# Edge stage of a graph network: edge features transposed in 32x32 squares by VectorE, sources broadcast by DMA

## The chip, the cores and the metric

The kernel runs on 1 core of one Trainium2 chip. The metric is the device time of one execution in microseconds (us). Of the kernel before, three runs are shown: 1167.19, 1169.51 and 1170.66 us, median 1169.51.

## What is computed

One layer of a graph network over 50,000 nodes with 128 features and 12,500 edges, in fp32. Every edge has a source `src` (the node that it adds to), a `dst` (the node that it reads), and 3, 5 and 32 features. Cut to what matters, with `idx_i = src` and `idx_j = dst`:

```python
h = relu(layernorm(x))
xx, xs, xp, xd = resmlp_0(h), resmlp_1(h)[idx_j], resmlp_2(h)[idx_j], resmlp_3(h)[idx_j]
gs, gp, gd = rbf @ w_rs, (rbf @ w_rp) * pij, (rbf @ w_rd) * dij      # rbf: 32 features, pij: 3, dij: 5
s = xx + segment_sum(gs * xs, idx_i)
p, d = segment_sum(gp * xp, idx_i), segment_sum(gd * xd, idx_i)
pa, pb = split(p @ w_pp); da, db = split(d @ w_pd)
y = s + (pa * pb).sum() + (da * db).sum()
out = x + resmlp_4(y)
```

where `resmlp(x) = silu(x + silu(silu(x) @ w1 + b1) @ w2 + b2) @ wout`.

## The kernel before, in words

The program has three stages, one after the other. The **first stage** (0 to about 368 us) normalises the nodes, stores them in DRAM as `node_h`, computes resmlp_0 of most of them, and sorts the edges by source with two passes of indirect DMAs on POOL. Its result is the DRAM table `edges_by_src`: 12,544 rows of 42 words of 4 bytes (source, dst, 3 + 5 features, 32 features), 98 tiles of 128 edges. The **edge stage** (about 368 to 856 us) is what the change touches. The **final stage** (856 us to the end) is resmlp_4 over all nodes.

The edge stage works on 25 groups (G) of 4 tiles (TB), so of 512 edges, the last one of 2 tiles. There is no planner: each engine has a list of calls written out by hand, a loop over k, in which the work of group k is mixed with that of group t = k - 1. The engines meet through semaphores.

- **SP** issues the DMAs. `load_group` (L57) brings the rows of a group with one edge per partition: `er` (first 10 words, for 512 edges), `rb` (last 32 words) and `nxt` (the source of the next edge, 512 single words). Groups 0 and 1 are loaded at the end of the first stage. Then SP loads `border_keys` with three small DMAs (L1211), counted by the semaphore `keys_in`, and in step k stores the border sums of group k - 2 (L1198, L1199) and loads group k + 2. All of these go through one queue (q1).
- **POOL** gathers the nodes of the dst (`yin<-node_h,er`, L72) and adds the finished rows to `node_sums` (L1247).
- **PE** runs `tensor`. In step k: `up(k,0)` (L1593), `gates(k)` (L1619, L1621: the 32 features times three weights), `halves(t,0)` (L1667, L1668), in step 0 also `key_rows` (L1712: a transpose of `border_keys`, which waits for `keys_in`), `sums(t-1)` (L1706), `up(k,1)`, `down(k,0)` (L1603), `seg(t)`, and so on down to `rows_T(k+1)` (L1570), `edges_T(k+1)` (L1582, L1583), `outp(k,2)` (L1638), `inner(t,3)` (L1676, L1677) and `borders(t)` (L1689 to L1695).
- `edges_T` on PE (L1573) transposes `er` and `rb` of a group, 128x128 each, into BANK_A, so that the features lie on 32 partitions per tile. `edges_T` on ACT (L1458) copies them out of PSUM: `eR` (L1466), `eA` (L1467) and two copies of `eA` with rows set to zero, `ePD` (L1468, L1469). `up(k,0)` waits for these copies, since it writes the same bank.
- `seg(t)` on PE (L1642) makes for each tile the products of the edges' 3 and 5 features (L1652, two halves of `quad`) and, with `pick_src` as weights, a 128x128 block in which every row holds the sources of the tile (L1656). Each of these uses 32 rows of the array.
- **DVE** in step k: `residual`, `masks(t)` (L1298), where `same` (L1308) compares the block of sources in PSUM with the edge's own source in `er`, and `gram` (L1311) multiplies it onto the products; `rows`, `message`, `products`, `take_h(k+1)` (L1271), `message(k,2)` (L1296), `products(t,3)` (L1342), `sums(t)` (L1352, L1355). In step 0 it begins with `key_masks` (L1358), which waits for `key_rows` and for `keys_in`.

The order that matters is in `vector` and `tensor`:

```python
            take_h(k + 1)          # DVE
            message(k, 2)
...
            rows_T(k + 1)          # PE
            edges_T(k + 1)
            outp(k, 2)
```

## Time and profile before

| | |
|---|---|
| median of 3 runs | 1169.51 us |
| profiled execution: span from the first to the last instruction | 1167.6 us (no other time of it is shown) |
| PE busy | 1106.1 us, 95% |
| ACT busy | 757.1 us, 65% |
| DVE busy | 635.5 us, 54% |
| POOL busy | 463.0 us, 40% |
| edge stage, one step of a whole group | 18.08 us |

PE is TensorE's matmuls, PEld its weight loads, SPq the DMAs that SP issues. An fp32 matmul is recorded as two instructions ("x2"), and the profile models the ends of matmuls, so a duration such as 0.60 us reaches into the next instruction; the distance from the start of one to the start of the next is what an instruction costs on PE. The chain of waits follows the work that ended last back from the last instruction.

### The profile page before, as it was taken

Reading aid. Unit: us, or ns where it says so; the run is one execution under the profiler, and the core shown is the slowest. Engines: PE = TensorE matmul, PEld = TensorE weight load, DVE = VectorE, ACT = ScalarE, POOL = GpSimd, SP = SyncE. Lnnn points to the kernel's source line nnn. Section 1 sums busy time; section 2 is a strip of 40 time slices with the busy share of each in tenths; the row PEclk is TensorE's granted clock in tenths of the full one; section 3 lists DMA queues with packets and bytes.
Section 4 is the critical chain, followed back from the end, with each engine's and each line's share of the span. In section 5 each row is a group of like instructions: output and inputs, shape, how many; then the busy total and the mean of one; then the engine's idle time right before and its main releaser. Section 6 shows DMA issues by size and latency. Waiting matters only on the chain.

```text
span 1167.6 us, 22917 instructions
## 1 busy us (share of the span) xinstructions
PE 1106.1 (95%) x6787; PEld 751.3 (64%) x6787; DVE 635.5 (54%) x2304; ACT 757.1 (65%) x1423; POOL 463.0 (40%) x426
## 2 busy tenths in 40 slices
PE   3799999899995899999999999999889999999998
PEld 2466766677773466676666666767556666666665
DVE  9999885878762456556565565565512222222222
ACT  2488999789995565655655656555356666666654
POOL 3077773077775346556555565563500000000000
PEclk9999999999998899999999999999999999999999
DMA  8389779477755033333333333334357878888774
GB/s 261 106 264 346 255 254 314 167 232 252 259 180 141 25 66 60 64 59 47 55 49 54 59 50 54 58 44 87 60 176 253 263 254 263 260 249 264 266 241 149
DMA packets 163582, 191.51 MB, mean 164 GB/s; under 512 B 58050, under 2 KB 82538, under 8 KB 163359
## 3 DMA queue, kind: packets, MB, share of 16 engines
q1 hardware_dynamic: 125166, 145.35, 40.6%
q0 software_dynamic: 24208, 19.29, 10.1%
q10 hardware_dynamic: 14112, 25.70, 5.8%
q8 instruction: 47, 0.77, 0.3%
q14 instruction: 49, 0.40, 0.1%
HBM read 94.06 MB, written 96.20 MB: 163 GB/s over the span
## 4 chain that ended last, share of the span: by engine, by line
PE 86%; DVE 9%; DMA 2%; issue 2%; ACT 1%; POOL 0%; SPq 0%; POOLq 0%; ACTq 0%; DVEq 0%
PE bank L1035 8%; PE quad L1023 7%; PE bank L1593 6%; PE bank L858 6%; PE quad L841 6%; PE quad L1027 5%; PE bank L1603 5%; PE bank L1667 4%; PE quad L848 4%; PE bank L1635 4%; PE bank L1668 4%; PE quad L1012 3%; DVE stat L521 2%; PE quad L826 2%; DVE onehot L633 2%; PE quad L1677 2%
## 5 line engine op out<-in xcount | busy, mean ns | idle before, releaser
L1247 POOL DMA_INDIRECT node_sums<-rowout,row_i x98 | 154.9, 1581 | 188.1 <-ACT rowout L1509 165.6
L952 DVE TENSOR_TENSOR rowout<-bank,xin 128x512 f32<-128x512 f32 x98 | 67.8, 692 | 248.7 <-PE bank L1035 248.7
L1035 PEld LDWEIGHTS bank<-wo_sb,s 128*128 128x128 f32 x784 | 102.8, 192 | 47.7 <-issue 47.7
L1280 DVE SCALAR_TENSOR_TENSOR h<-bank,b_sb,hT 128x512 f32<-128x512 f32 (+1 forms) x75 | 55.5, 740 | 138.9 <-PE bank L1603 138.9
L465 POOL DMA_INDIRECT edges_by_src<-pay,rank_i x98 | 99.8, 1019 | 70.9 <-DVE rank_i L662 42.0
L465 POOL DMA_INDIRECT edges_by_low<-pay,rank_i x98 | 98.3, 1003 | 62.1 <-DVE rank_i L662 32.2
L858 PEld LDWEIGHTS bank<-wo_sb,s 128*128 128x128 f32 x720 | 94.7, 192 | 42.9 <-issue 42.9
L751 ACT ACTIVATE xn<-xin,nbias,rnorm 128x128 f32<-128x128 f32 x216 | 103.6, 491 | 14.8 <-DVE nbias L572 14.7
L72 POOL DMA_INDIRECT yin<-node_h,er x98 | 94.7, 967 | 38.1 <-issue 29.2
L1035 PE MATMUL bank<-wo_sb,s 128*128 128x128 f32 x784 | 103.5, 275 | 0.9 <-DVE rowout L952 0.9
L1023 PE MATMUL quad<-s,w_sb 128*128 128x512 f32 x196 | 101.7, 601 | 0.1
L521 DVE BATCH_NORM_STATS2 stat<-xin 128x6 f32<-128x128 f32 x392 | 99.5, 282 | 0.0
L841 PE MATMUL quad<-s,w_sb 128*128 128x512 f32 x188 | 98.5, 606 | 0.1
L858 PE MATMUL bank<-wo_sb,s 128*128 128x128 f32 x720 | 94.9, 275 | 0.0
L1456 ACT ACTIVATE s<-h 128x512 f32<-128x512 f32 (+1 forms) x75 | 46.6, 621 | 73.1 <-DVE h L1280 73.1
L1488 ACT COPY AB<-bank 128x512 f32<-128x512 f32 x98 | 58.1, 593 | 50.4 <-PE bank L1668 50.3
L973 ACT ACTIVATE s<-quad,b_sb 128x512 f32<-128x512 f32 x98 | 67.3, 687 | 26.8 <-PE quad L1023 26.7
L650 DVE SCALAR_TENSOR_TENSOR picked<-bank,onehot 128x256 bf16<-128x256 f32 (+1 forms) x196 | 67.4, 387 | 31.0 <-PE bank L814 28.2
L1593 PE MATMUL bank<-s,w_sb 128*128 128x512 f32 (+1 forms) x150 | 79.1, 609 | 3.2 <-ACT ePD L1469 3.0
L965 ACT ACTIVATE s<-quad 128x512 f32<-128x512 f32 x74 | 44.2, 597 | 54.5 <-PE quad L1012 45.5
L1027 PE MATMUL quad<-s,w_sb 128*128 128x512 f32 x148 | 75.6, 593 | 0.0
L1603 PE MATMUL bank<-s,w_sb 128*128 128x512 f32 (+1 forms) x150 | 75.5, 585 | 0.1
(208 smaller groups left out, 2313.2 us busy)
## 6 DMA issues: line engine op xcount, KB each, us to landing
xin<-in_x_dram SPq DMA_DIRECT2D x196, 256.0 KB, 3.2
node_h<-xn SPq DMA_DIRECT2D x98, 256.0 KB, 2.8
yin<-node_sums SPq DMA_DIRECT2D x98, 256.0 KB, 3.6
out_dram<-rowout ACTq DMA_DIRECT2D x98, 256.0 KB, 3.5
node_sums<-rowout SPq DMA_DIRECT2D x90, 256.0 KB
border_sums_by_tile<-border_sums SPq DMA_DIRECT2D x24, 256.0 KB, 2.0
node_sums<-zeros SPq DMA_DIRECT2D x8, 256.0 KB
edges_by_low<-pay,rank_i POOLq DMA_INDIRECT x98
```

The costliest lines, as they stand in the source:

```text
L72: pool.indirect_dma_start(out=xg[:, s, j, :], out_offset=None, in_=x, in_offset=bass.IndirectOffsetOnAxis(ap=er[:, s, j, 1:2].bitcast(mybi ...
L465: nc.gpsimd.indirect_dma_start(out=ps.dram, out_offset=bass.IndirectOffsetOnAxis(ap=rank_i[:, t:t + 1], axis=0), in_=pay[:, t, :], in_offs ...
L521: last = nc.vector.bn_stats(stat[:, b % 32, j, :], xin[:, s, j, :])
L751: ins = nc.scalar.activation(xn[:, b % 4, j, :], xin[:, s, j, :], ACT.Relu, bias=nbias[:, q, i:i + 1], scale=rnorm[:, q, i:i + 1])
L841: nc.tensor.matmul(BANK_A[:, :], w1_sb[:, m, :], s1[:, (k - 1) % 3, :], start=True, stop=True).then_inc(a_done, 1)
L858: last = nc.tensor.matmul(BANK_O[:, j * P:(j + 1) * P], s3[:, (k - 3) % 3, j * P:(j + 1) * P], wo_sb[:, m, :], start=True, stop=True)
L1023: nc.tensor.matmul(BANK_A[:, :], w1_sb[:, m, :], s1[:, s, :], start=True, stop=True).then_inc(a_done, 1)
L1027: nc.tensor.matmul(BANK_X[s][:, :], w2_sb[:, m, :], s2[:, s, :], start=False, stop=True, skip_group_check=True).then_inc(b_done, 1)
L1035: last = nc.tensor.matmul(BANK_O[:, j * P:(j + 1) * P], s3[:, s, j * P:(j + 1) * P], wo_sb[:, m, :], start=True, stop=True)
L1247: nc.gpsimd.indirect_dma_start(out=ysum, out_offset=bass.IndirectOffsetOnAxis(ap=row_i[:, t % 2, j:j + 1], axis=0), in_=urow[:, t % 2, j, ...
L1593: nc.tensor.matmul(BANK_A[:, 0:e], w1_sb[:, MLP[m], :], s1[:, k % 2, 0:e], start=True, stop=True).then_inc(a_done, 1)
L1603: nc.tensor.matmul(BANK_B[:, 0:e], w2_sb[:, MLP[m], :], s2[:, m, 0:e], start=True, stop=True).then_inc(b_done, 1)
```

## The change

The 32 partitions per tile are made in another way. Each tile's rows are loaded once more, all 42 words of them, 32 edges on 32 partitions and four such blocks side by side (`rq`, one DMA per tile in place of `rb`). VectorE's 32x32 transpose turns `rq` into `eR` and `eA` directly (`features_T`), so PE's two transposes and two of ACT's four copies go; the two `ePD` copies now read `eA`. The block of sources no longer comes from `pick_src` matmuls: at the start of the stage one DMA copies the first word of all 12,544 rows of `edges_by_src` into a contiguous DRAM row (`src_row`), and then one DMA per group (`load_src_row`) reads 512 words of it to all 128 partitions (`srow`, two buffers). `keys_in` counts the `src_row` copy too. The matmul operand `pick_src` and the clearing of `er` in the first stage go, and the final stage reuses semaphores of the first (with their earlier counts added to its waits). The core of the diff (step by step; the rest is names and counts):

```diff
-def load_group(eng, by_src, er, rb, nxt, s, k, TB, T, done, indices):
-    P, W = er.shape[0], by_src.shape[1]
-    C = W - rb.shape[3]
+def load_group(eng, by_src, er, rq, nxt, s, k, TB, T, done, indices):
+    P, C, Q = er.shape[0], er.shape[3], er.shape[0] // TB
     start, n = k * TB * P, min(TB, T - k * TB)
     rows = by_src[start:start + n * P, :].rearrange("(t p) w -> p t w", p=P)
-    eng.dma_start(er[:, s, 0:n, 0:C], rows[:, :, 0:C]).then_inc(indices, 16)
-    eng.dma_start(rb[:, s, 0:n, :], rows[:, :, C:W]).then_inc(done, 16)
+    eng.dma_start(er[:, s, 0:n, :], rows[:, :, 0:C]).then_inc(indices, 16)
+    for t in range(n):
+        tile = by_src[start + t * P:start + (t + 1) * P, :].rearrange("(q r) w -> r q w", r=Q)
+        eng.dma_start(rq[t * Q:(t + 1) * Q, s, :, :], tile).then_inc(done, 16)
...
-        er = sb("er", [P, U, TB, Q])
-        rb = sb("rb", [P, U, TB, NRBF])
+        er = sb("er", [P, U, TB, C_RBF])
+        rq = sb("rq", [P, U, P // Q, W])
...
+    srow = sb("src_in_every_row", [P, 2, BLOCK])
...
+    src_row = nc.dram_tensor("edge_src_row", [1, T * P], fp32, kind="Internal").ap()
...
+                    sp.wait_ge(quads_T, k - U + 1)
...
+        def load_src_row(k):
+            if k < G:
+                s, e = k % 2, tiles(k) * P
+                if k >= 2:
+                    sp.wait_ge(same_done, k - 1)
+                sp.dma_start(srow[:, s, 0:e], src_row[0:1, k * BLOCK:k * BLOCK + e].to_broadcast([P, e])).then_inc(srow_in[s], 16)
...
+        with nc.allow_non_contiguous_dma(reason="one word of each row"):
+            sp.dma_start(src_row[0, :].rearrange("(t p) -> t p", p=P), by_src[0:T * P, 0:1].rearrange("(t p) w -> t (p w)", p=P),
+                         allow_slow_non_contiguous=True).then_inc(keys_in, 16)
         with nc.allow_non_contiguous_dma(reason="first and last key of each tile"):
             for n, row in enumerate((0, P - 1, P)):
...
             load(k + 2)
+            if k == 0:
+                sp.wait_ge(keys_in, 64)
+                load_src_row(0)
+            load_src_row(k + 1)
...
+        def features_T(k):
+            if k < G:
+                q, s = k % 2, k % U
+                if k == 0:
+                    dve.wait_ge(first_index_in, 16)
+                dve.wait_ge(rows_in[s], rows_there(k))
+                if k >= 2:
+                    dve.wait_ge(seg_ps, k - 1)
+                    dve.wait_ge(g_ps, k - 1)
+                nc.vector.transpose(eR[:, q, :].rearrange("p (q r) -> p q r", r=Q), rq[:, s, :, W - Q:W])
+                nc.vector.transpose(eA[:, q, :].rearrange("p (q r) -> p q r", r=Q), rq[:, s, :, 0:Q]).then_inc(quads_T, 1)
...
-                dve.wait_ge(seg_ps, t + 1)
+                dve.wait_ge(srow_in[t % 2], 16 * (t // 2 + 1))
                 if t >= 1:
                     dve.wait_ge(u_ps, t)
                     dve.wait_ge(t_done, TB * t)
                     dve.wait_ge(bd_ps, t)
-                nc.vector.tensor_tensor(same[:, 0:n, :], quad[:, 0:n, 2 * P:3 * P], src.unsqueeze(2).to_broadcast([P, n, P]),
-                                        ALU.is_equal).then_inc(same_done, 1)
+                nc.vector.tensor_tensor(same[:, 0:n, :], srow[:, t % 2, 0:n * P].rearrange("p (t e) -> p t e", t=n),
+                                        src.unsqueeze(2).to_broadcast([P, n, P]), ALU.is_equal).then_inc(same_done, 1)
+                dve.wait_ge(seg_ps, t + 1)
...
-            dve.wait_ge(keys_in, 48)
+            dve.wait_ge(keys_in, 64)
...
+        features_T(0)
         take_h(0)
...
             take_h(k + 1)
+            features_T(k + 1)
             message(k, 2)
...
-                act.wait_ge(eT_ps, k + 1)
+                act.wait_ge(quads_T, k + 1)
                 if k >= 2:
                     act.wait_ge(seg_ps, k - 1)
-                    act.wait_ge(g_ps, k - 1)
-                nc.scalar.copy(eR[:, q, :], BANK_A[:, P:2 * P])
-                nc.scalar.copy(eA[:, q, :], BANK_A[:, 0:P])
-                nc.scalar.activation(ePD[:, q, 0, :], BANK_A[:, 0:P], ACT.Identity, scale=p_rows[:, 0:1])
-                nc.scalar.activation(ePD[:, q, 1, :], BANK_A[:, 0:P], ACT.Identity, scale=d_rows[:, 0:1]).then_inc(eT_done, 1)
+                nc.scalar.activation(ePD[:, q, 0, :], eA[:, q, :], ACT.Identity, scale=p_rows[:, 0:1])
+                nc.scalar.activation(ePD[:, q, 1, :], eA[:, q, :], ACT.Identity, scale=d_rows[:, 0:1]).then_inc(eT_done, 1)
...
-        def edges_T(k):
-            if k < G:
-                s = k % U
-                if k == 0:
-                    pe.wait_ge(first_index_in, 16)
-                pe.wait_ge(rows_in[s], rows_there(k))
-                if k >= 1:
-                    pe.wait_ge(s2_done, 3 * k)
-                nc.tensor.transpose(BANK_A[:, 0:P], er[:, s, :, :].rearrange("p t c -> p (t c)"), ident[:, :])
-                nc.tensor.transpose(BANK_A[:, P:2 * P], rb[:, s, :, :].rearrange("p t c -> p (t c)"), ident[:, :]).then_inc(eT_ps, 1)
...
-                if m == 0:
-                    pe.wait_ge(eT_done, k + 1)
-                else:
+                if k or m:
...
-                pe.wait_ge(eT_done, k + 1)
+                pe.wait_ge(quads_T, k + 1)
...
+                pe.wait_ge(eT_done, t + 1)
                 if t + 1 < G:
                     pe.wait_ge(gate_done, t + 2)
                 else:
                     pe.wait_ge(prod_done, TB * t)
                 for j in range(tiles(t)):
                     rows = slice(j * Q, (j + 1) * Q)
-                    nc.tensor.matmul(quad[:, j, 0:2 * P], eA[rows, q, :], ePD[rows, q, :, :].rearrange("p a e -> p (a e)"),
-                                     start=True, stop=True, skip_group_check=True)
-                for j in range(tiles(t)):
-                    rows = slice(j * Q, (j + 1) * Q)
-                    last = nc.tensor.matmul(quad[:, j, 2 * P:3 * P], pick_src[rows, :], eA[rows, q, :], start=False, stop=True, skip_group_check=True)
+                    last = nc.tensor.matmul(quad[:, j, 0:2 * P], eA[rows, q, :], ePD[rows, q, :, :].rearrange("p a e -> p (a e)"),
+                                            start=True, stop=True, skip_group_check=True)
                 last.then_inc(seg_ps, 1)
...
-            pe.wait_ge(keys_in, 48)
+            pe.wait_ge(keys_in, 64)
...
-        edges_T(0)
...
             rows_T(k + 1)
-            edges_T(k + 1)
```

Where instructions move, the order of the program shows it at three places. First the queue of SP at the start of the edge stage, before the change, from the load of group 1 on (names of semaphores in brackets; `edges_by_src` is the table of edges in DRAM):

```order
L64 DMA er<-edges_by_src 128x4x10
L65 DMA rb<-edges_by_src 128x4x32
L66 DMA nxt<-edges_by_src 128x4x1
L1211 DMA border_keys<-edges_by_src 98x1 x3
L64 DMA er<-edges_by_src 128x4x10
L65 DMA rb<-edges_by_src 128x4x32
L66 DMA nxt<-edges_by_src 128x4x1
L64 DMA er<-edges_by_src 128x4x10
L65 DMA rb<-edges_by_src 128x4x32
```

and with the change:

```order
L64 DMA er<-edges_by_src 128x4x10
L67 DMA rq<-edges_by_src 32x4x42 x4
L68 DMA nxt<-edges_by_src 128x4x1
L1225 DMA edge_src_row<-edges_by_src 12544x1
L1229 DMA border_keys<-edges_by_src 98x1 x3
L64 DMA er<-edges_by_src 128x4x10
L67 DMA rq<-edges_by_src 32x4x42 x4
L68 DMA nxt<-edges_by_src 128x4x1
L1206 DMA src_in_every_row<-edge_src_row 128x512 [waits e_keys_in]
L1206 DMA src_in_every_row<-edge_src_row 128x512
L64 DMA er<-edges_by_src 128x4x10
L67 DMA rq<-edges_by_src 32x4x42 x4
```

The `rb` load of each group has become four, the copy of 12,544 single words stands ahead of `border_keys` and ahead of the load of group 2, and the load of group 3 stands behind a wait for `keys_in`.

Second, PE in a whole step, around `seg(t)`, of before:

```order
L1593 MATMUL bank<-s,w_sb 128x512
L1603 MATMUL bank<-s,w_sb 128x512
L1652 MATMUL quad<-ePD,eA 128x256 x4
L1656 MATMUL quad<-eA,pick_src 128x128 x4
L1667 MATMUL bank<-wpp_sb,mT 128x256
L1668 MATMUL bank<-wpd_sb,mT 128x256
L1593 MATMUL bank<-s,w_sb 128x512
```

and with the change, where the row of `pick_src` is gone and nothing takes its place:

```order
L1615 MATMUL bank<-s,w_sb 128x512
L1625 MATMUL bank<-s,w_sb 128x512
L1675 MATMUL quad<-ePD,eA 128x256 x4
L1687 MATMUL bank<-wpp_sb,mT 128x256
L1688 MATMUL bank<-wpd_sb,mT 128x256
L1615 MATMUL bank<-s,w_sb 128x512
```

Third, DVE in a whole step, from `take_h` to the first `residual` of the next step, with the change; before, the two rows STREAM_TRANSPOSE were not there, and `same` read `quad`:

```order
L1293 COPY hT<-quad 128x512
L1306 STREAM_TRANSPOSE eR<-rq 128x128
L1307 STREAM_TRANSPOSE eA<-rq 128x128
L1332 TENSOR_TENSOR msg<-bank,gate 128x512
L1379 TENSOR_TENSOR prod<-quad,AB 128x256
L1389 TENSOR_TENSOR allsum<-prod 128x512
L1392 TENSOR_TENSOR allsum<-allsum,msg 128x512
L1316 SCALAR_TENSOR_TENSOR h<-bank,b_sb,hT 128x512
L1344 TENSOR_TENSOR same<-src_in_every_row,er 128x512
```

Both transposes stand between `take_h`, on which the next step's matmuls rest, and the last `message` of this step.

## Rows read from the trace of the kernel before

**Rows 1.** The page: busy time by engine; the chain that ended last.

```profile
PE 1106.1 (95%) x6787; PEld 751.3 (64%) x6787; DVE 635.5 (54%) x2304; ACT 757.1 (65%) x1423; POOL 463.0 (40%) x426
...
PE 86%; DVE 9%; DMA 2%; issue 2%; ACT 1%; POOL 0%; SPq 0%; POOLq 0%; ACTq 0%; DVEq 0%
```

**Rows 2.** Busy time in stretches (us): PE, PEld, DVE, ACT, POOL; granted clock; DMA share; GB/s.

```profile
369.00:385.00 16.00, 5.09 (x32) 3.02 (x33) 0.69 (x1) 2.16 (x6) 10.52 (x11) 0.50 0.47 72
...
386.00:395.30 9.30, 7.79 (x28) 3.67 (x26) 5.71 (x14) 5.25 (x12) 3.96 (x5) 1.00 0.12 35
539.00:557.08 18.08, 18.08 (x139) 12.26 (x135) 10.62 (x25) 10.48 (x21) 10.17 (x8) 1.00 0.34 54
```

**Rows 3.** The timeline of PE in one whole step: start, us, what.

```profile
544.58 0.71 PE L1652 MATMUL quad<-ePD,eA 32*128 32x256 f32 x8
545.12 0.40 PE L1656 MATMUL quad<-eA,pick_src 32*128 32x128 f32 x8
545.45 0.70 PE L1667 MATMUL bank<-wpp_sb,mT 128*128 128x256 f32 x2
...
554.21 0.27 PE L1582 MATMUL bank<-ident,er 128*128 128x128 f32 x1
...
554.42 1.06 PE L1638 MATMUL bank<-wo_sb,s 128*128 128x128 f32 x8
...
558.11 0.73 PE L1619 MATMUL quad<-eR,wr_sb 32*128 32x128 f32 x16
```

**Rows 4.** The timeline of DVE in the same step.

```profile
554.41 0.69 DVE L1271 COPY hT<-quad 128x512 f32<-128x512 f32 x1
555.52 0.69 DVE L1296 TENSOR_TENSOR msg<-bank,gate 128x512 f32<-128x512 f32 x1 [0.42 <-PE bank L1638]
556.13 0.41 DVE L1342 TENSOR_TENSOR prod<-quad,AB 128x256 f32<-128x256 f32 x1
```

**Rows 5.** The timeline of all engines at the start of the edge stage.

```profile
368.41 0.37 SPq L64 DMA_DIRECT2D er<-edges_by_src  x1
...
371.63 1.35 SPq L1211 DMA_DIRECT2D border_keys<-edges_by_src  x3
...
377.88 1.09 PE L1570 MATMUL quad<-ident,yin 128*128 128x128 f32 x4 [12.72 <-DMA yin<-node_h,er]
...
385.00 0.40 PE L1712 MATMUL bank<-ident,border_keys 98*98 98x98 f32 x1
...
393.64 0.63 ACT L1440 ACTIVATE s<-hT 128x512 f32<-128x512 f32 x1 [0.76 <-DVE hT L1271]
...
395.26 1.10 PE L1593 MATMUL bank<-s,w_sb 128*128 128x512 f32 x2 [0.97 <-ACT ePD L1469]
```

**Rows 6.** The page: a group of DVE: count, busy, mean ns, idle before.

```profile
L521 DVE BATCH_NORM_STATS2 stat<-xin 128x6 f32<-128x128 f32 x392 | 99.5, 282 | 0.0
```

**Rows 7.** DMA issues: KB each, median us from issue to landing.

```profile
nxt<-edges_by_src SPq DMA_DIRECT2D x24, 2.0 KB, 2.2
```

**Rows 8.** The timeline of SP's queue in the same whole step.

```profile
539.89 0.33 SPq L1198 DMA_DIRECT2D border_sums_by_tile<-border_sums  x1
540.26 0.43 SPq L1199 DMA_DIRECT2D border_s_sums_by_tile<-border_s_sums  x1
540.79 0.40 SPq L64 DMA_DIRECT2D er<-edges_by_src  x1
```

**Rows 9.** DMA queues, stretch 542.95 to 543.6: packets, MB, share of 16 engines.

```profile
q1 hardware_dynamic: 741, 0.03, 71.1%
```

**Rows 10.** The same, stretch 369.4 to 373.

```profile
q1 hardware_dynamic: 3268, 0.18, 63.3%
```

**Rows 11.** The same, stretch 240 to 360 (POOL's queue).

```profile
q0 software_dynamic: 2880, 1.94, 6.9%
```

**Rows 12.** The same, stretch 379 to 391 (POOL's queue).

```profile
q0 software_dynamic: 317, 0.66, 18.9%
```

**Rows 13.** The same, stretch 418 to 436.08 (POOL's queue).

```profile
q0 software_dynamic: 704, 0.52, 21.1%
```

More of the change, by code:

```diff
@@ L157, in gnn_kernel @@
         row_4 = sb("row_in_group", [P, 1])
-        pick_src = sb("pick_src", [P, P])
         w1_sb = sb("w1_sb", [P, NMLP, F])
@@ L190, in rows_there @@
         def rows_there(k):
-            return 48 * (k // U + 1) - (0 if k % U else 16)
+            each = 16 * (TB + 2)
+            short = 16 * (TB - (T - k * TB)) if k == G - 1 and T - k * TB < TB else 0
+            return each * (k // U + 1) - (0 if k % U else 16) - short
         gathered = [sem(f"gathered{i}") for i in range(U)]
@@ L354, in h_made @@
                 eng.wait_ge(nrm_a, NB)
+            ring_x_in = [(x_in[s], 16 * len(range(s, NB, NX))) for s in range(4 + ND, 8 + ND)]
+            ring_stored = [(h_stored[s], 16 * len(range(s, NB, 4))) for s in range(4)]
             late_x_in = [(x_in[s], 16 * len(range(s, NB, NX))) for s in range(4, 4 + ND)]
@@ L447, in sync @@
                     for g in (0, 1):
-                        load_group(sp, by_src, er, rb, nxt, g, g, TB, T, rows_in[g], rows_in[g] if g else first_index_in)
+                        load_group(sp, by_src, er, rq, nxt, g, g, TB, T, rows_in[g], rows_in[g] if g else first_index_in)
             def gpsimd(pool):
@@ L904, in fsem @@
                 return sem("f_" + nm)
-            x_in = [fsem(f"x_in{i}") for i in range(4)]
+            x_in, x_before = zip(*ring_x_in)
+            stored, stored_before = zip(*ring_stored)
             y_in = [fsem(f"y_in{i}") for i in range(4)]
-            stored = [fsem(f"stored{i}") for i in range(4)]
             yT_done, s1_done, a_done, s2_done, b_done, s3_done, o_done, row_done = (fsem(s) for s in (
@@ L1087, in edge_phase @@
     htab, by_src, ysum, psum, quad, sb = (env[n] for n in ("htab", "by_src", "ysum", "psum", "quad", "sb"))
-    ident, trash_by_side, trash_by_tile, p_rows, d_rows, pick_src = (
-        env[n] for n in ("ident", "trash_by_side", "trash_by_tile", "p_rows", "d_rows", "pick_src"))
+    ident, trash_by_side, trash_by_tile, p_rows, d_rows = (
+        env[n] for n in ("ident", "trash_by_side", "trash_by_tile", "p_rows", "d_rows"))
     w1_sb, w2_sb, wo_sb, b1_sb, b2_sb, wr_sb, wpp_sb, wpd_sb = (
@@ L1162, in edge_phase @@
                          "sum_done", "u_in_psum", "u_done", "row_steps", "rows_done"))
+    quads_T = sem("edge_features_T")
+    srow_in = [sem(f"src_row_in{i}") for i in range(2)]
     key_ps, key_done, item_rows, item_ps, item_c, item_steps, item_done = (
```

33 lines of the change are left out of this document (15 added, 18 removed).

## The prediction

> **What bounds the kernel now.** I read the page's busy times and the chain of waits first. PE is busy 95% of the span and carries 86% of the chain that ended last [rows 1], so a change counts here if it shortens PE's list or makes PE wait. The busy time by stretches then says how tight the edge stage is: in a whole step of 18.08 us PE is busy all of it at the full clock, DVE for 10.62 and ACT for 10.48 us [rows 2]. The timeline of PE in that step shows no idle time in front of any matmul. So in a whole step each instruction taken from PE is worth its distance from start to start, as long as nothing else becomes late. The start of the stage is different: from 369 to 385 us PE is busy for 5.09 of 16 us and its clock is granted at 0.50, the 1.2 GHz level [rows 2]. There PE waits for data, and what DMAs do decides.
>
> **What is taken from PE.** The four `pick_src` matmuls of a group start at 545.12 and the next instruction at 545.45 [rows 3]: 0.33 us, 25 times, 8.3 us. The two transposes start at 554.21 and `outp` at 554.42 [rows 3]: 0.21 us, 24 times, 5.0 us; those of group 0 lie ahead of the stall below and are counted at nothing. Together **-13.3 us**. Nothing replaces them on PE. L1652 ahead of them, with 256 columns instead of 128, takes 0.54 us from start to start [rows 3]; so 128 columns are 0.21 us and 0.12 us is fixed. If the fixed part stays behind with the instructions that remain, 25 x 0.21 + 5.0 = 10.3 us is the low end of this term.
>
> **What becomes late when PE is faster.** The first suspect is DVE. The two squares (32x32 transposes, 128 columns each) have no row. The nearest is 282 ns for an instruction that reads 128x128 [rows 6]; I take 0.28 us each, 0.56 us per group, with ends of 0.15 us and, for a copy of 512 columns, 0.69 us [rows 4]. They stand after `take_h`, which ends at 555.10, and the last `message` starts at 555.52 because it waits for PE [rows 4]; so 0.42 of the 0.56 us fall into idle time and `message` is 0.1 to 0.2 us later. Behind it is `products(t,3)`, which ends at 556.54 [rows 4], and the next step's `gates` on PE, at 558.11 [rows 3], waits for it: 1.57 us of slack, 0.21 of it used by PE's gain. Even two squares of 0.69 us cost less than the slack that is left (0.96 of 1.36 us). Counted at nothing. ACT loses two copies of the four and has idle time in every step. `same` reads SBUF instead of PSUM and no longer waits for `seg`; `gram` behind it still does, so nothing starts earlier that PE waits for.
>
> DMA: each group now moves the same number of small rows, with 168 bytes where `rb` had 128, and 128 rows of 2 KB more. DMA's share is 0.34 in a whole step [rows 2]. The new broadcast is issued once `same` of step k is through and is read in step k + 2, some 30 us later; the loads of rows are two groups ahead. SP issues four more DMAs per step; at some 0.45 us each that is 1.8 us in 18.08. All of this hides behind PE. The operation that leaves DVE in the first stage, the clearing of `er` on POOL and the shared semaphores of the final stage are counted at nothing: no wait and no work on PE changes with them.
>
> **The wait that is added.** `key_rows` on PE runs at 385.00 [rows 5] and waits for `keys_in`, which now counts the copy of 12,544 single words. Behind it on PE is `up(0,1)`, the whole rest of step 0; `key_masks` on DVE waits for the same, and behind it are all `residual` of step 0. So the stage stands until the copy has landed. When is that?
>
> - Start. SP issued the first six loads from 368.41 to 371.63 [rows 5], 0.54 us each. Two of them become eight smaller ones; DMAs of 128 rows take 0.37 and 0.53 us to the next [rows 8], mean 0.45. So 371.63 - 2 x 0.54 + 8 x 0.45 = 374.15.
> - Duration. The copy is one packet per word. The nearest rows are the loads of single words and short rows on the same queue: 741 packets in 0.65 us, 1.14 per ns [rows 9], and with the gaps between issues 3268 in 3.6 us, 0.91 per ns [rows 10]. The mean of both, 1.02 per ns, gives 12.3 us; the two ends 11.0 and 13.8 us. These land in SBUF and the copy writes DRAM. The nearest DRAM writes are the sort's scatters: 0.069 x 16 engines x 120 us = 132 engine-us for 2880 packets [rows 11]. A POOL DMA of 128 rows has about 32 packets (317 for ten gathers [rows 12]), so these are 90 DMAs, 11,520 rows of 168 bytes, 11.5 ns each. One engine has 784 words; at 11.5 ns that is 9 us. So writing DRAM need not be slower, and I take 12.3 us. The far end is the adding DMAs, which read DRAM before they write it: 0.211 x 16 x 18.08 = 61 engine-us [rows 13], less four gathers at 0.189 x 16 x 12 / 10 = 3.6 [rows 12], leaves 46.5 for 512 rows, 91 ns each, and 71 us for the copy.
> - Landing. The three `border_keys` DMAs stand behind it, 1.35 us [rows 5], and land 2.2 us after issue, as `nxt` does [rows 7]. 374.15 + 12.3 + 1.35 + 2.2 = 390.0 us, so PE waits until 390.0 instead of going on at 385.0: **+5.0 us**.
> - Clock. PE began at 377.88 [rows 5] and was granted 1.2 GHz until about 385, 7.1 us later [rows 2]. If it stays there again for as long after the stall, it does the work of 3.6 us in 7.1. PE is busy 7.79 of 9.3 us there [rows 2], so some **+3.0 us**; ends 0 and 3.6.
> - In step 1 `up(1,0)` waited for the last copy of ACT until 395.26; now it needs only the silu that starts at 393.64 and ends 0.63 us later [rows 5], with the same 0.2 us of delay 394.47: **-0.8 us**.
>
> What else queues behind the copy: the load of group 2 and, behind SP's wait, that of group 3. Group 2 lands some 5 us after the stall ends, its four gathers take 5 us more, and its `rows_T` comes 24 us after `key_rows`. Hidden, at every duration of the copy, since that step moves too.
>
> **Sum.** -13.3 - 0.8 + 5.0 + 3.0 = -6.1 us. The profiled execution shows 1167.6 us of span and no other time; the median of the runs is 1169.5, 1.9 above it. -6.1 on it is **1163.4 us**.
>
> The Trainium skill ("DMA: Bandwidth & Descriptors", table of rules, and "VectorE: DVE Perf Modes", "The three transpose paths") speaks against this copy: a strided last dimension becomes one descriptor per element, and a copy that transposes by strides is put at 19 times the 1309 ns of the hardware's transpose of 128x128. By that figure, an estimate, 12,544 of 16,384 elements take 19.0 us instead of 12.3, and the sum would be +0.6 us. By the first rule the trace agrees, 741 packets of 40 bytes at the mean [rows 9]; for the second no row of before has such a copy.
>
> **The rivals.** All differ in the price of one word in the copy; it is the one thing that no row shows. A difference from no change that a measurement of this kernel can tell is about 0.3%, 3.5 us.
>
> - *Gain and stall cancel.* The total is within 3.5 us of before when the copy takes 14.9 to 21.9 us, so 19 to 28 ns per word and engine. A mechanism for it: single words written next to each other in DRAM go slower than scattered rows of 168 bytes. At 19.0 us the stall is 11.7 us and the time 1170.1 us. For it: the engines' share was already 0.71 at the fastest rate of the loads [rows 9], so there is little room for dearer words. Against it: the 11.5 ns of the scatters. The same total would come if the saving on PE were 10.3 us and the copy 13.8.
> - *The stall outgrows the gain.* Each word costs DRAM a read before its write, as in the adding DMAs. From 28 ns per word it decides the sign. At 32 ns, between 11.5 and 91 by ratio, the copy takes 25.1 us, the stall 17.8, and the time is 1176.2 us; at 91 ns it would be 1222 us. For it: 91 ns [rows 13]. Against it: those rows are read by instruction, not because they are short.
> - *The stall is hidden.* The copy at 11.0 us, `border_keys` issued while it still runs, no loss of clock: 387.35, so +2.35 - 14.1 = -11.7 us, 1157.8 us.
>
> **How the numbers follow.** Faster: 0.55, most of it between 1158 and 1166; within 0.3%: 0.18; slower: 0.27, which has the open end. The likeliest is the forecast, 1163.4. Its own range, with the copy between 11.0 and 14.9 us and the clock term between 0 and 3.6, is 1159 to 1167. The range for 8 in 10 runs from 1156, a little below the hidden stall, to the slower case with 37 ns per word, 1180 us.
>
> **What would show it.** In a whole step the distance of equal matmuls should be 17.54 instead of 18.08 us, and PE without idle time there; the squares 0.28 us each in front of `message`. At the start PE idle in front of `key_rows` until about 390 us, released by a DMA, a granted clock of 0.5 behind it for some us, and `up(1,0)` less than 10 us after. Wrong if a step stays above 17.7 us (DVE or a DMA is late), if `key_rows` is not what PE waits for, or if the copy takes over 15 us: then the sign follows from its duration alone.

## The result, and the profile after

| | before | changed |
|---|---|---|
| median | 1169.1 us (4 runs, 1167.19 to 1170.66) | 1193.01 us (4 runs, 1192.27 to 1193.69) |
| span of the profiled execution | 1167.6 us | 1191.5 us |
| whole step of the edge stage | 18.08 us | 17.64 us |
| from the load of `er` to `key_rows` on PE | 16.59 us | 51.87 us |

The ratio is 1.0207, 95% interval [1.0192, 1.0221]: slower, by 24 us, where a gain of 6 was forecast. PE does less and waits more. The page of the changed kernel (busy time, queue q1, the chain of waits):

```profile
PE 1094.4 (92%) x6541; PEld 735.0 (62%) x6541; DVE 639.7 (54%) x2353; ACT 751.1 (63%) x1373; POOL 466.7 (39%) x425
...
PE 84%; DVE 8%; SPq 4%; DMA 2%; issue 1%; ACT 1%; POOL 0%; POOLq 0%; ACTq 0%; DVEq 0%
```

PE's busy time fell by 11.7 us against [rows 1], but SP's queue, which had no part in the chain, now holds 4% of it, some 48 us of the span. Where, the stretches say (columns as in [rows 2]):

```profile
369.00:385.00 16.00, 0.00 (x0) 0.00 (x0) 0.51 (x2) 0.00 (x0) 7.66 (x8) 0.50 0.39 26
385.00:409.00 24.00, 4.60 (x30) 2.54 (x30) 0.69 (x1) 3.46 (x7) 0.00 (x0) 0.57 0.75 13
409.00:418.00 9.00, 0.00 (x0) 0.00 (x0) 0.00 (x0) 0.00 (x0) 0.00 (x0) 0.50 0.31 12
418.00:429.30 11.30, 10.67 (x27) 4.87 (x27) 5.97 (x17) 3.93 (x7) 7.44 (x8) 0.77 0.37 97
570.00:587.64 17.64, 17.64 (x125) 11.62 (x124) 10.77 (x27) 10.22 (x20) 10.30 (x8) 1.00 0.42 71
```

From 369 to 418 us PE works 4.6 us at a granted clock of 0.50 to 0.57, and the DMAs move 12 to 26 GB/s, against 72 in the first of these stretches before [rows 2]. The last row is a whole step: full of PE's work, as in [rows 2], and 0.44 us shorter. The start, first SP's queue, then PE:

```profile
366.22 0.37 SPq L64 DMA_DIRECT2D er<-edges_by_src  x1
...
372.14 0.62 SPq L1225 DMA_DIRECT2D edge_src_row<-edges_by_src  x1
372.80 36.92 SPq L1229 DMA_DIRECT2D border_keys<-edges_by_src  x3
```

```profile
390.11 1.09 PE L1606 MATMUL quad<-ident,yin 128*128 128x128 f32 x4 [27.15 <-DMA yin<-node_h,er]
...
418.09 0.40 PE L1732 MATMUL bank<-ident,border_keys 98*98 98x98 f32 x1 [21.85 <-DMA border_keys<-edges_by_src]
...
429.31 1.12 PE L1615 MATMUL bank<-s,w_sb 128*128 128x512 f32 x2
```

The three key loads took SP 1.35 us to issue before [rows 5]; now 36.92, of which it stands 36.05 us at the second. The last of them is issued at 409.3, and `key_rows` starts at 418.09, 8.7 us later, where a small load landed in 2.2 us before [rows 7]. PE has waited 21.85 us for it. And something that the prediction had not priced: `rows_T(0)`, which waits for the first gathers on POOL's own queue, comes at 390.11, 23.89 us after `er` instead of 9.47.

Accounting between the two profiled executions, 23.9 us: first stage -2.19 (`er` issued at 366.22 for 368.41); `er` to `key_rows` +35.28; `key_rows` to the border sums of group 0, at the end of step 1 (the row of `border_weights` on PE, 411.22 before, 444.87 after) +0.56; from there to the first `yin` of the final stage (854.74, 878.54) -9.85; the rest +0.10.

### The profile page after: what moved, and what is told of

It is laid out like the page before. It is cut to its first block, busy times and chain, and to the rows that moved or that the text cites. A ratio compares the mean times of both kernels' runs of the same rounds, so it can differ in the third digit from the quotient of the medians.

```text
span 1191.5 us, 22589 instructions
## 1 busy us (share of the span) xinstructions
PE 1094.4 (92%) x6541; PEld 735.0 (62%) x6541; DVE 639.7 (54%) x2353; ACT 751.1 (63%) x1373; POOL 466.7 (39%) x425
## 4 chain that ended last, share of the span: by engine, by line
PE 84%; DVE 8%; SPq 4%; DMA 2%; issue 1%; ACT 1%; POOL 0%; POOLq 0%; ACTq 0%; DVEq 0%
PE bank L1038 7%; PE quad L1026 7%; PE bank L1615 6%; PE bank L861 6%; PE quad L844 6%; PE bank L1625 5%; PE quad L1030 5%; PE bank L1687 4%; PE quad L851 4%; PE bank L1657 4%; PE bank L1688 4%; SPq L1229 3%; PE quad L1015 3%; PE quad L829 2%; DVE stat L525 2%; DVE onehot L637 2%
## 5 line engine op out<-in xcount | busy, mean ns | idle before, releaser
L1026 PE MATMUL quad<-s,w_sb 128*128 128x512 f32 x196 | 100.5, 594 | 0.6 <-ACT s L976 0.4
L844 PE MATMUL quad<-s,w_sb 128*128 128x512 f32 x188 | 98.5, 606 | 0.1
L1487 ACT ACTIVATE s<-bank,b_sb 128x512 f32<-128x512 f32 (+1 forms) x75 | 51.0, 680 | 42.3 <-PE bank L1615 42.3
```

The lines of the kernel that those rows point to most:

```text
L844: nc.tensor.matmul(BANK_A[:, :], w1_sb[:, m, :], s1[:, (k - 1) % 3, :], start=True, stop=True).then_inc(a_done, 1)
L1026: nc.tensor.matmul(BANK_A[:, :], w1_sb[:, m, :], s1[:, s, :], start=True, stop=True).then_inc(a_done, 1)
```

## The experiments

The chip matters for reading them. Twelve of the experiments ran on two chips on which every kernel, the one before too, spends 60 to 67 us more in the first stage (`er` issued at 429 to 436 us); the other three (l, m and f_again) ran on one that is like the first. So totals are set only against the kernel before on the same chip, and the rest is told in distances from the issue of `er`. The columns, all in us: from `er` to `rows_T(0)`; "held", the time for which SP's queue was held behind the copy (the row of the next DMAs less what they took without it); from `er` to `key_rows`; from `er` to the border sums of group 0 (the expected texts call these, and the masks of group 0, those of step 0; both stand in step 1). "Held" ends when SP can issue again, not when the copy has landed, so it is less than the copy's own time.

| kernel | `rows_T(0)` | held | `key_rows` | border sums |
|---|---|---|---|---|
| before, first chip | 9.5 | - | 16.6 | 42.8 |
| changed, first chip | 23.9 | 35.6 | 51.9 | 78.7 |
| before_here | 9.6 | - | 16.7 | 53.5 |
| after_here | 23.5 | 34.9 | 53.7 | 81.0 |
| a_copy_alone | 34.3 | 38.3 | 50.2 | 78.2 |
| k_half_words | 33.1 | 15.8 | 40.2 | 72.2 |
| i_write_alone | 47.1 | 59.8 | 84.9 | 112.5 |
| b_spaced (64 B) | 21.0 | 19.9 | 28.8 | 56.9 |
| l_spaced_512 | 19.0 | 15.4 | 26.1 | 52.3 |
| m_write_64_bytes | 12.5 | 8.7 | 19.6 | 46.1 |
| c_to_sbuf | 12.5 | 8.0 | 19.6 | 49.2 |
| d_rows_from_squares | 9.4 | - | 15.6 | 51.1 |
| d_again | 9.4 | - | 15.6 | 52.8 |
| h_picks_back | 9.5 | - | 15.7 | 51.3 |
| e_keys_first | 9.4 | 34.4 | 15.6 | 70.2 |
| f_copy_by_sbuf | 9.4 | 8.4 | 15.6 | 40.7 |
| f_again | 9.3 | 8.9 | 15.5 | 40.4 |

### The copy alone, and what of it is dear

a, b, c, i, k, l, m are the kernel before with nothing added but a copy ahead of the key loads, which `key_rows` and `key_masks` wait for. a: the copy of the change.

```diff
+            sp.dma_start(src_row[0, :].rearrange("(t p) -> t p", p=P), by_src[0:T * P, 0:1].rearrange("(t p) w -> t (p w)", p=P),
+                         allow_slow_non_contiguous=True).then_inc(keys_in, 16)
             for n, row in enumerate((0, P - 1, P)):
```

> The kernel before with nothing but the copy of 12,544 words added, at the same place in SP's queue, counted in keys_in. Theory (the copy makes the whole loss): SP's next DMA is held some 36 us and key_rows starts at about 417 us instead of 385, the time rises by 33 to 37 us to about 1203, whole steps stay at 18.08 us. Rival (the loss needs the other new DMAs as well, the rq loads or the broadcasts): key_rows before 400 and less than 15 us more.

1268.0 us against 1248.8 for the kernel before there: 19 us more, and not 33 to 37, on a chip on which the kernel before has a wait of its own in step 0 (see the second part below). SP's queue:

```profile
435.36 0.58 SPq L1211 DMA_DIRECT2D edge_src_row<-edges_by_src  x1
435.99 39.68 SPq L1215 DMA_DIRECT2D border_keys<-edges_by_src  x3
```

The queue is held 38.3 us and `key_rows` comes 50.2 us after `er`: the copy by itself makes the whole stall, with nothing else of the change in the kernel. b writes each word 64 bytes behind the last, c writes them to SBUF:

```diff
-    src_row[0, :].rearrange("(t p) -> t p", p=P)
+    src_row[:, 0:1].rearrange("(t p) w -> t (p w)", p=P)
```

with `src_row` of [T * P, 16] words in b, and in c

```diff
-    src_row[0, :].rearrange("(t p) -> t p", p=P)
+    src_tile[0:T, :]
```

> As a_copy_alone, but the words are written 64 bytes apart in DRAM instead of side by side. Theory N (neighbouring words share a line in DRAM, and each write waits for the one before): the copy falls to the rate of the loads, 11 to 14 us, key_rows at 388 to 392, time 1170 to 1176. Theory W (any single word written to DRAM is dear, some 46 ns per engine): key_rows at about 417 as in a_copy_alone, time about 1203. Theory R (reading or issuing so many words is what is slow): the same as W.

> As a_copy_alone, but the words are written to SBUF, 98 partitions of 128 words; the reads are the same. Theories N and W (the DRAM write is what is slow): the copy takes 11 to 15 us, key_rows at 388 to 393, time 1170 to 1177. Theory R (reads or issue): key_rows stays at 410 or later, time 1197 or more.

```profile
438.70 21.27 SPq L1215 DMA_DIRECT2D border_keys<-edges_by_src  x3
```

```profile
437.75 9.36 SPq L1215 DMA_DIRECT2D border_keys<-edges_by_src  x3
```

(1250.8 and 1241.3 us.) c came out as expected: reading the words and issuing their packets holds the queue for no more than 8.0 us, and the rest of a's 38.3 comes with the write to DRAM. b lies between its theories: 19.9 us, so a part of the cost goes when the words don't lie side by side, and a part stays. i takes the read away instead: the words come out of every second word of an SBUF tile.

```diff
-    by_src[0:T * P, 0:1].rearrange("(t p) w -> t (p w)", p=P)
+    words[0:T, 0:2 * P:2]
```

> The kernel before with a copy of 12,544 single words out of an SBUF tile (every second word of 98 partitions) into the same row in DRAM, where they lie next to each other: the write side without the scattered read from DRAM. If the write of words side by side is the dear part, the load of the keys behind it is held up about as long as in a_copy_alone, 30 to 37 us, and key_rows comes 43 to 51 us after er. If read and write together are needed (each cheap alone, as c_to_sbuf showed of the read): under 15 us, key_rows under 28 us after er.

```profile
438.12 61.19 SPq L1216 DMA_DIRECT2D border_keys<-edges_by_src  x3
```

1304.4 us against 1243.9: 59.8 us held, beyond both expectations. The write alone is enough; why it is dearer than with the read ahead of it was not settled. k copies half of the words (`TH = T // 2` for `T` on both sides).

> The kernel before with the copy of the first 49 of the 98 tiles, 6,272 words side by side. If the duration goes by the number of words, half of it goes: the keys' load is held up 14 to 19 us and key_rows comes 26 to 33 us after er (50.2 with all the words). If a fixed part or the queue's depth is most of it, over 25 us held up.

```profile
432.79 17.11 SPq L1216 DMA_DIRECT2D border_keys<-edges_by_src  x3
...
462.01 1.09 PE L1575 MATMUL quad<-ident,yin 128*128 128x128 f32 x4 [36.33 <-DMA yin<-node_h,er]
```

1258.7 us. The hold goes by the number of words (15.8 us for half of them, 38.3 for all), but the gathers' delay doesn't: `rows_T(0)` is as late as with all of them (33.1 and 34.3 us), so `key_rows`, which stands behind it on PE, comes at 40.2 and not by 33. Among the kernels that write words side by side from DRAM, what goes with the delay is how many of the first group's four gathers POOL had issued when the copy was issued: one in a and k; three in the changed kernel, 23.9 us; all four in e below, 9.4 us, as without a copy. No run tested this by itself, and why the delay is as long as it is stays open. l spaces the words by 512 bytes; m writes the first 64 bytes of each row to 64 bytes of their own:

```diff
-    src_row[0, :].rearrange("(t p) -> t p", p=P)
-    by_src[0:T * P, 0:1].rearrange("(t p) w -> t (p w)", p=P)
+    src_row[:, :].rearrange("(t p) w -> t p w", p=P)
+    by_src[0:T * P, 0:16].rearrange("(t p) w -> t p w", p=P)
```

> As the spaced copy, with 512 bytes instead of 64 between one written word and the next. If words only have to keep out of each other's 64 bytes, nothing more is won: the keys' load held up 18 to 23 us (20.4 there), key_rows 27 to 31 us after er. If what they share is longer than 64 bytes, the hold falls to 8 to 12 us, as with an SBUF target (8.5 us), key_rows under 22 us after er. If a word that stands alone in DRAM is dear in itself and more so far from its neighbour: over 25 us.

> As the spaced copy, but each of the 12,544 pieces is the first 64 bytes of an edge's row instead of its first word, written to 64 bytes of its own: as many pieces as before, sixteen times the bytes, and no 64 bytes written in part. If the price is that of writing a part of 64 bytes in DRAM: 8 to 12 us held up, as with an SBUF target. If it goes by pieces that go to DRAM, whatever their size: 18 to 23 us, as with spaced words.

1177.2 and 1173.1 us against 1168.8. l lies between its expectations (15.4 us), a little better than 64 bytes. m is clear; SP's rows of l and then of m:

```profile
370.33 16.75 SPq L1215 DMA_DIRECT2D border_keys<-edges_by_src  x3
```

```profile
372.34 10.06 SPq L1215 DMA_DIRECT2D border_keys<-edges_by_src  x3
```

As many pieces, sixteen times the bytes, to DRAM, and the queue is held 8.7 us, as with an SBUF target. So neither the number of pieces nor DRAM as a target is dear by itself, but 4 bytes written there at a time, side by side most of all. What DRAM does with such a word, and why words 512 bytes apart still hold the queue 15.4 us, is not settled. The Trainium skill ("DMA: Bandwidth & Descriptors", "Specifications") has transfers under 512 bytes do a read-modify-write. The words bear out that a short write can cost much more than its bytes; the 64 bytes of m, well under 512, show no such cost. The measurement decides: that limit is not where this copy's cost begins.

### Which wait the stall is

The kernel before and the changed one, on the chip of the following runs.

> The kernel before, unchanged, profiled on the chip on which the three other runs of this call are made. No theory differs on it; it gives the stage times to set theirs against. Expected if this chip is like the first: er issued near 366 to 369 us, key_rows on TensorE 16.6 us later, a whole edge step of 18.08 us, span near 1167. If it is like the chip of the first four experiments: first stage near 432 us, span near 1247.

> The changed kernel, unchanged, on the same chip as the kernel before. Theory N (the words of the copy lie next to each other in DRAM and each write waits for the one before it): the copy's cost belongs to the kernel and not to the chip, so from the load of er to key_rows 48 to 54 us here too against 16 to 18 before, a whole step 0.44 us shorter, and the ratio of the totals 1.015 to 1.025. Rival: the 36 us stall of the first profile was in part the chip's; then key_rows comes under 40 us after er and the ratio lies under 1.012.

1248.23 us (one run; 1247.76 median of 17) and 1261.25. `key_rows` comes 53.7 us after `er` instead of 51.9, so the stall belongs to the kernel, but the ratio is 1.0093 [1.0059, 1.0127], under the 1.015 that was expected. The kernel before has on this chip a wait of its own in step 0, whose releaser the profile can't name:

```profile
461.59 1.56 ACT L1478 COPY gate<-quad 128x512 f32<-128x512 f32 x3 [9.87 <-remote]
```

The profile writes "remote" for it. From `key_rows` to the border sums of group 0 the kernel before takes 36.8 us here and 26.2 on the first chip; the changed kernel takes 27.3 and 26.8 and shows no such wait behind its stall. These 10.6 us are about what the gap between the two kernels is smaller by (23.9 us there, 13.5 here). c, which shows no such wait either, is even below the kernel before. That the wait passes unseen inside the stall is likely and not shown. The ratio of the first chip, 1.0207, is free of it.

e issues the key loads ahead of the copy and lets PE and DVE wait for them alone; only SP's broadcasts of the sources wait for the copy.

```diff
-            sp.dma_start(src_row[0, :].rearrange("(t p) -> t p", p=P), by_src[0:T * P, 0:1].rearrange("(t p) w -> t (p w)", p=P),
-                         allow_slow_non_contiguous=True).then_inc(keys_in, 16)
             for n, row in enumerate((0, P - 1, P)):
...
+            sp.dma_start(src_row[0, :].rearrange("(t p) -> t p", p=P), by_src[0:T * P, 0:1].rearrange("(t p) w -> t (p w)", p=P),
+                         allow_slow_non_contiguous=True).then_inc(words_in, 16)
...
-                sp.wait_ge(keys_in, 64)
+                sp.wait_ge(words_in, 16)
...
-            pe.wait_ge(keys_in, 64)
+            pe.wait_ge(keys_in, 48)
```

> The changed kernel with the three loads of keys issued ahead of the copy of the words, and key_rows and key_masks waiting for the keys alone; only SyncE's broadcasts of the sources wait for the copy, through a semaphore of its own. Theory 1, the copy's own duration is the whole damage: key_rows comes when the first gather has landed (rows_T(0), 20 to 24 us after er), TensorE does up(1,0) at about 28 to 34 us after er, and the wait moves on to the masks of step 0, whose broadcast can land only when the copy is done (45 to 50 us after er); since the masks stand late in a step, some 10 to 20 us of the 32 are won back and the total is 1.000 to 1.012 of before. Theory 2, the wait for the keys was only the first of equal waits (gathers and the loads behind the copy are as late): the total stays within 4 us of the changed kernel, 1.017 to 1.023 of before.

1252.1 us, ratio 1.0038 [1.0017, 1.0059], as theory 1 expected. The copy here has a semaphore of its own, so that SP's rows show when it landed:

```profile
438.20 0.58 SPq L1230 DMA_DIRECT2D edge_src_row<-edges_by_src  x1
438.82 34.86 SPq L64 DMA_DIRECT2D er<-edges_by_src  x1
...
486.15 0.82 SPq L1207 DMA_DIRECT2D src_in_every_row<-edge_src_row  x2
```

From issue to landing the copy takes 48.0 us (438.20 to SP's release at 486.15), 13.6 more than it holds the queue. PE's rows at the waits of the first two steps, and then one of DVE:

```profile
446.36 0.40 PE L1733 MATMUL bank<-ident,border_keys 98*98 98x98 f32 x1
...
465.64 1.12 PE L1607 MATMUL quad<-ident,yin 128*128 128x128 f32 x4 [11.17 <-DMA yin<-node_h,er]
...
493.70 2.04 PE L1626 MATMUL bank<-s,w_sb 128*128 128x512 f32 x2 [15.08 <-DVE h L1317]
```

```profile
490.38 0.69 DVE L1345 TENSOR_TENSOR same<-src_in_every_row,er 128x512 f32<-128x512 f32 x1 [16.11 <-DMA src_in_every_row<-edge_src_row]
```

`key_rows` is on time. The wait has moved: 11.17 us for the second group's gathers and 15.08 us for DVE, which stands at `same` of group 0 for 16.11 us until the broadcast is there. The first gathers, issued some 1.5 us further ahead of the copy than in after_here (the copy 7.4 instead of 5.9 us after `er`), came in time; the second group's, issued behind it, were caught. So gathers on POOL's queue are late once their packets stand beside the copy's.

### Without the dear copy

d leaves the copy out. SP stores rows 0, 32, 64 and 96 of the transposed squares, which are the sources, and broadcasts them.

```diff
+                sp.wait_ge(quads_T, k + 1)
+                sp.dma_start(src_row[0, k * BLOCK:k * BLOCK + e].rearrange("(t p) -> t p", p=P),
+                             eA[0:(tiles(k) - 1) * Q + 1:Q, s, :]).then_inc(srow_out, 16)
+                sp.wait_ge(srow_out, 16 * (k + 1))
```

> The changed kernel without the copy of words: the sources of a group are row 0 of each 32-partition block of eA, so SP stores these four rows of 512 bytes to the DRAM row in each step and then broadcasts them; keys_in counts border_keys alone. If the copy is the whole loss and the rest of the change is worth 0.44 us per step: whole steps 17.64 us, key_rows at about 385, no wait in front of masks; 24 x 0.44 + 0.8 = 11.4 us less than before, ratio 0.990, about 1158. If the store, SP's two waits per step or the broadcast are late: steps above 17.7 us with DVE idle in front of same.

> A repeat, in more rounds, of the version without the copy, where SyncE stores the sources row from the transposed squares of each step. If the 0.4 us of each whole step is all there is (24 steps by 0.44 us = 10.6 us off, nothing put back), the ratio to the kernel before is 0.990 to 0.993 and a whole step takes 17.64 us. If the store, the wait for it and the broadcast stand in the way of a step, a whole step takes over 17.75 us and the ratio is over 0.994. If the 9 us for which VectorE and ScalarE stood still in step 0 of the first run of this kernel belong to the kernel and not to that execution, they show here again, and the ratio could fall to 0.983 without them.

1236.29 us, ratio 0.9911 [0.9884, 0.9939]; again 1235.57, 0.9902 [0.9875, 0.9928]. A whole step takes 17.64 us: the gain of the steps is there. In d_again nine of the 21 steps from the border sums of group 0 on take about 0.1 us more, 1.0 us in all, which is what the store, the wait and the broadcast can have put back. The unnamed wait in step 0 (9.7 and 10.9 us of ACT) is in the kernel before too, so it is no cost of d. h is d with four matmuls of the shape of the `pick_src` ones back on PE, their result not used:

```diff
+                    last = nc.tensor.matmul(quad[:, j, 2 * P:3 * P], ident[rows, :], eA[rows, q, :], start=False, stop=True, skip_group_check=True)
```

> The version without the copy, with the four small matmuls that copy the sources to all rows put back on TensorE (their result is not used). It splits the 0.44 us of a step. By the trace of the kernel before, four of them took 0.33 us, of which 0.10 came back when they went (the matmuls of L1675 to those of L1687: 0.64 us for 0.54): a whole step 17.64 + 0.23 = 17.87 us. If the transposes alone were worth the 0.44: 17.64; if the matmuls were: 18.08. The latter two would refute the split.

```profile
481.56 0.62 PE L1712 MATMUL bank<-AB,border_weights 128*6 128x256 f32 x8
...
499.42 0.62 PE L1712 MATMUL bank<-AB,border_weights 128*6 128x256 f32 x8
```

1235.2 us, and a step of 17.86: the picks are worth 0.22 us, which leaves the other 0.22 of the 0.44 to the transposes. f keeps the design of the change, keys first, but takes the words by way of SBUF:

```diff
-            sp.dma_start(src_row[0, :].rearrange("(t p) -> t p", p=P), by_src[0:T * P, 0:1].rearrange("(t p) w -> t (p w)", p=P),
+            sp.dma_start(src_tile[0:T, :], by_src[0:T * P, 0:1].rearrange("(t p) w -> t (p w)", p=P),
...
                 sp.wait_ge(words_in, 16)
+                sp.dma_start(src_row[0, :].rearrange("(t p) -> t p", p=P), src_tile[0:T, :]).then_inc(words_in, 16)
+                sp.wait_ge(words_in, 32)
```

> As the version with the keys first, but the words go from DRAM into an SBUF tile of 98 partitions (one tile of edges each), and from there one transfer of 98 rows of 512 bytes writes the sources row. If only single words written to DRAM are dear (c_to_sbuf: the keys' load held up 8.5 us instead of 36): from er to the border sums of step 0 on TensorE (the row of border_weights) 50 to 55 us against 53.5 for the kernel before on this chip and 70 with the keys first, and a ratio of 0.989 to 0.994. If reading single words is as dear once the keys and gathers no longer lie behind it, or the second transfer and the broadcast add a wait for the masks of step 0: over 58 us, and a ratio over 0.996.

> A repeat, in more rounds, of the version that copies the words by way of SBUF, keys first. If all that it wins is the 24 steps (0.41 us each, 9.9 us) and the 2 us of an earlier start: a ratio of 0.989 to 0.991. If it also takes away the 10 to 14 us for which ScalarE and VectorE wait in step 0 on the second chip (the kernel before and the version without the copy have that wait there, the first run of this version had none): 0.979 to 0.986 there; on a chip whose kernel before shows no such wait, 0.988 to 0.992.

1220.9 us, ratio 0.9824 [0.9787, 0.9861], and on the chip like the first **1154.13 us, ratio 0.9874 [0.9856, 0.9893]**: faster than both kernels, and better than expected both times. Neither of the two profiles has the unnamed wait of step 0, which the kernel before has on the first of these chips; that fits the better ratio there. What the wait is stays open.

```profile
373.85 1.00 SPq L1231 DMA_DIRECT2D src_by_tile<-edges_by_src  x1
374.89 9.42 SPq L64 DMA_DIRECT2D er<-edges_by_src  x1
...
386.79 0.49 SPq L1238 DMA_DIRECT2D edge_src_row<-src_by_tile  x1
388.46 0.82 SPq L1208 DMA_DIRECT2D src_in_every_row<-edge_src_row  x2
```

SP issues the copy to SBUF at 373.85 and gets past the wait for it by 386.79, so that copy landed within 12.9 us, against 48.0 for the words to DRAM in e. The store of 98 rows and its landing take 1.7 us (386.79 to the broadcast at 388.46). How the two copies run, by queue q1 from 375 to 384 us, the changed kernel first and f_again second:

```profile
q1 hardware_dynamic: 1966, 0.01, 23.7%
```

```profile
q1 hardware_dynamic: 12458, 0.05, 105.1%
```

1966 packets in 9 us against 12,458. The share of the 16 engines is only 23.7% in the slow one, so in this stretch most of what the copy waits for is not booked as the time of its packets; from 385 to 409 us, behind it, all DMAs together have 0.75 (the row of that stretch above).

## Why the prediction was wrong

**The step that failed is "Duration"**: 12.3 us for the copy, with 11.0 and 13.8 as ends. In the prediction's own sum, from the copy's issue at 372.14 to SP's release at 418.06, less 1.35 and 2.2 for the keys, it was 42.4 us, 54 ns for each of the 784 words that the prediction gives an engine, beyond even the 37 ns with which the range ended. SP's queue stood for 35.6 us of it. The wait that is added came out at +35.3 us for +5.0. That is 30.3 us, and the whole miss is 30.0 (+23.9 for -6.1): the other terms cancel, with 3.0 us less taken from PE, 1.2 less for the clock and 2.2 from the first stage. The step's argument, "So writing DRAM need not be slower", came from the sort's scatters [rows 11]: rows of 168 bytes. For larger pieces it holds: m wrote 12,544 pieces of 64 bytes to DRAM while holding the queue no longer than an SBUF target (8.7 and 8.0 to 8.9 us), and into SBUF f_again moved 12,458 packets in 9 us, 1.38 per ns, no slower than the 1.14 and 0.91 of [rows 9, 10]. What it missed is the other property of the new transfer, words of 4 bytes side by side. The rival "gain and stall cancel" named single words next to each other and priced them at 19.0 us; the rival "the stall outgrows the gain" had the sign and, with 32 ns, too small a price. Words kept apart still held the queue 7 to 11 us longer than pieces of 64 bytes, so being next to each other is not all of it; whether each word costs DRAM a read before its write no run shows. The Trainium skill's figure of 19 times ("VectorE: DVE Perf Modes", "The three transpose paths") gave the estimate of 19.0 us, less than half of what was measured; the skill gives it for a large stride on the destination's side, and here the destination's words lie side by side.

**A second failure: what is behind the copy on other queues.** The prediction listed the loads of groups 2 and 3 and did not name POOL's gathers. `rows_T(0)` came 14 us late (23.89 instead of 9.47). In the changed kernel that cost nothing, since the keys came later still; but e shows that with the keys out of the way the second group's gathers and the broadcast stop PE instead. The Trainium skill ("DMA: Bandwidth & Descriptors", "Queues, rings and completion order") says that each engine takes turns between its queues packet by packet, and ("Back-pressure in remote DMA"), of another kind of transfer, that "Stalled writes stall the source SDMA engine's other queues too". By the first the gathers would take turns with the copy's words; by the second, if it held for local writes too, they would stand with them. Which it is here no run shows.

Term by term:

- *What is taken from PE*: -13.3, low end 10.3. Measured -9.85 from the border sums of group 0 on, and with the 0.44 of the step ahead of them 10.3, the low end. L1652's successor (L1675) keeps the fixed part when its 128-column neighbours go, as the low end had it:

```profile
575.16 0.71 PE L1675 MATMUL quad<-ePD,eA 32*128 32x256 f32 x8
575.80 0.70 PE L1687 MATMUL bank<-wpp_sb,mT 128*128 128x256 f32 x2
```

  0.64 us from start to start for 0.54 [rows 3]; so 0.44 us per step, not 0.54, and 21 equal distances of 17.64 us (9.2 us) with a shorter tail rather than 24 or 25 full steps.
- *The squares*: 0.28 us, counted at nothing. Right: 0.30 and 0.27, of which PE notices nothing.

```profile
585.37 0.30 DVE L1306 STREAM_TRANSPOSE eR<-rq 128x128 f32<-128x128 f32 x1
585.59 0.27 DVE L1307 STREAM_TRANSPOSE eA<-rq 128x128 f32<-128x128 f32 x1
585.79 0.65 DVE L1332 TENSOR_TENSOR msg<-bank,gate 128x512 f32<-128x512 f32 x1
```

- *Start of the copy*: 5.74 us after `er` predicted, 5.92 measured. Right.
- *Which wait*: `key_rows` is what PE waits for, released by a DMA. Right, but `rows_T(0)` waits ahead of it.
- *Clock*: +3.0. From `key_rows` to `up(1,0)` 11.22 us instead of 10.26 (less than 10 was forecast), though the 0.8 us for ACT is gone: +1.8. The stretch behind the stall had a granted clock of 0.77 where 386.0 to 395.3 had 1.00 [rows 2]; PE had done nothing for over 20 us ahead of it.
- *Steps and DMAs behind PE*: right; 17.64 us with PE busy all of it, and d shows nearly the same with one more store and wait per step.

In f_again, with the keys first and the copy by way of SBUF, the kernel takes 14.7 us less than before (1154.13 against 1168.8): `er` to the border sums 40.44 instead of 42.81, then 9.89 less, and 1.9 from a first stage that varies by as much (`er` at 366.48 in l and 368.49 in m, which both have the first stage of the kernel before). So some 12.3 us are the design's. What the prediction said of PE's work held at its low end; the price of one transfer turned the sign.

## What to carry to other kernels

Price a transfer by the size of the piece that it writes and by where the piece lies, not by its count of pieces alone: pieces of 64 bytes, or words into SBUF, held the queue a quarter as long as single words side by side in DRAM. Read such a price from the copy's own semaphore: the time for which its queue is held is less (35 us of 48 here). Where single words must be gathered into a DRAM row, collect them in SBUF and store rows. And when a transfer is slow, look at every queue with work at that time, not only at what waits for its semaphore: keys moved ahead of it gained 9 us of a stall of 35, since gathers and the broadcast were late as well.

## What the runs showed of the hardware

- 12,544 words of 4 bytes from DRAM to neighbouring words of DRAM held the queue 34 to 38 us, and took 48.0 us to land (e), against at most 12.9 into SBUF (f_again). Held: 64 bytes apart 19.9, 512 bytes apart 15.4, into SBUF 8.0 to 8.9, as pieces of 64 bytes 8.7; from SBUF to neighbouring words 59.8.
- SP stood at the first (e, f) or the second DMA behind such a copy until most of it was done: in the changed kernel 13,209 packets of its queue began between the copy's issue and 409.3, and 2,034 more by 418.06. So such a copy is a wait for whatever SP issues next, loads of other groups among them.
- Gathers on POOL's queue took a median of 20.3 us to land beside the copy (five in the stretch from 373.5 to 390), against 2.4 to 2.5 before; half of the copy delayed them as much as all of it (33.1 and 34.3 us from `er` to `rows_T(0)`).
- Two chips show 60 to 67 us more in the first stage and, in some kernels, a wait of 9 to 15 us of ACT and DVE in step 0 (4.5 and 9.1 in k). The same change measured 1.0207 on one chip and 1.0093 on another: a ratio holds with the chip's own other waits in it.
